# Left-over rows of each expert in 32-row fp32 tails beside the 128-row slots

## The reference

```
c0   = per-batch 64x64 mix of x + bias               (stage 0, "cond")
logits = c0 @ gate_w                                  (8 experts)
top 2 experts of each row, softmax over the two logits -> w0, w1
x1   = x + w0 * (c0 @ expert_w[e0]) + w1 * (c0 @ expert_w[e1])     (1024 x 1024 each)
c1   = grouped convolution of x1 (9 taps) + bias      (stage 2)
out  = x1 + c1 @ weight.T + gated LoRA of c1          (stage 2)
```

## Time and profile before

| | |
|---|---|
| median of the runs | 840.09 us |
| profiled execution | 842.59 us, of which the span is 840.8 us |
| mean granted TensorE clock | 0.995 |
| TensorE matmul busy | 820.3 us (98%) |
| VectorE / ScalarE / GpSimd busy | 399.5 / 216.5 / 86.8 us |
| slot and main product, L1353 | 848 low-row matmuls = 53 x 16 |
| DMA | 149.32 MB, mean 178 GB/s |

### The profile page before, as it was taken

The page is one execution under the profiler, slowest core; times in us unless marked ns, Lnnn a source line. Parts: engine busy times, 40 slices in busy tenths (PEclk is TensorE's granted clock), DMA queues, the critical chain, the costliest instruction groups (busy, mean ns, idle before and its releaser), DMA issues.

```text
span 840.8 us, 12876 instructions
## 1 busy us (share of the span) xinstructions
PE 820.3 (98%) x4286; PEld 678.5 (81%) x4287; DVE 399.5 (48%) x919; ACT 216.5 (26%) x335; POOL 86.8 (10%) x136
## 2 busy tenths in 40 slices
PE   8999899999999999999999999999999999999997
PEld 6555588888888888888888888789888888988886
DVE  1388750251513304233042150466766776777883
ACT  2344341342524314243142251310001000101200
POOL 1000111011101111011101112021111111110000
PEclk9999999999999999999999999999999999999999
DMA  9998489373554634546255253584564456432056
GB/s 288 351 325 308 178 291 417 121 253 134 168 194 169 217 100 162 200 138 248 80 179 202 87 184 108 189 257 102 137 149 114 103 144 151 101 84 67 1 196 204
DMA packets 61801, 149.32 MB, mean 178 GB/s; under 512 B 6944, under 2 KB 23600, under 8 KB 60848
## 3 DMA queue, kind: packets, MB, share of 16 engines
q1 hardware_dynamic: 41104, 93.41, 33.7%
q0 software_dynamic: 9968, 36.19, 14.7%
q10 hardware_dynamic: 10704, 19.41, 6.1%
HBM read 100.74 MB, written 39.85 MB: 167 GB/s over the span
## 4 chain that ended last, share of the span: by engine, by line
PE 85%; DMA 6%; DVE 3%; issue 2%; ACT 2%; SPq 1%; ACTq 1%; POOL 0%; DVEq 0%; POOLq 0%
PE bank L1353 60%; PE bank L1392 6%; PE bank L1248 4%; PE bank L1401 4%; PE bank L1344 3%; DMA work<-in_expert_w 3%; PE bank L1408 3%; PE bank L1225 1%; DVE weights L977 1%; DMA work<-y_scratch,pos_c 1%; PE bank L1297 1%; PE bank L1272 1%; PE bank L1211 1%; DMA x1p<-res 1%; PE bank L1237 1%
## 5 line engine op out<-in xcount | busy, mean ns | idle before, releaser
L1353 PE MATMUL bank<-weights,l_hi 128*128 128x512 f32 x1696 | 524.4, 391 | 0.0
L1353 PEld LDWEIGHTS bank<-weights,l_hi 128*128 128x128 f32 x1696 | 319.4, 188 | 64.8
L1353 PE MATMUL bank<-weights,l_lo 128*128 128x512 f32 x848 | 336.1, 396 | 2.0 <-DVE l_lo L945 2.0
L1353 PEld LDWEIGHTS bank<-weights,l_lo 128*128 128x128 f32 x848 | 159.8, 188 | 34.7 <-issue 3.4
L945 DVE TENSOR_TENSOR l_lo<-bank,l_hi 128x512 fp32r<-128x512 f32 x37 | 25.6, 691 | 183.7 <-ACT l_hi L715 183.7
L977 DVE TENSOR_TENSOR weights<-work,weights 128x1024 fp32r<-128x1024 f32 x64 | 76.2, 1222 | 50.8 <-ACT weights L726 50.0
L726 ACT ACTIVATE weights<-work 128x1024 fp32r<-128x1024 f32 x64 | 65.3, 1055 | 41.9 <-DMA work<-in_expert_w 23.6
L572 POOL DMA_INDIRECT work<-c_scratch,idx x37 | 40.5, 1094 | 291.7 <-PE bank L1344 198.9
L1392 PE MATMUL bank<-conv_sb,x1p 128*128 128x128 f32 x512 | 59.8, 276 | 3.8 <-DMA x1p<-work 2.6
L1392 PEld LDWEIGHTS bank<-conv_sb,x1p 128*128 128x128 f32 x512 | 58.7, 192 | 4.3 <-DMA x1p<-work 2.8
L950 DVE TENSOR_TENSOR l_lo<-bank,l_hi 128x512 fp32r<-128x512 f32 x37 | 25.6, 691 | 68.7 <-ACT l_hi L720 68.7
(11 more groups left out here) (184 smaller groups left out, 528.9 us busy)
## 6 DMA issues: line engine op xcount, KB each, us to landing
work<-in_expert_w SPq DMA_DIRECT2D x68, 512.0 KB, 6.4
y_scratch<-work ACTq DMA_DIRECT2D x74, 256.0 KB, 2.1
res<-in_x SPq DMA_DIRECT2D x16, 512.0 KB, 15.3
c_scratch<-work SPq DMA_DIRECT2D x16, 512.0 KB, 3.5
res<-in_x_ph SPq DMA_DIRECT2D x14, 512.0 KB, 5.6
x1p<-res SPq DMA_DIRECT2D x112, 64.0 KB, 4.7
out<-res SPq DMA_DIRECT2D x14, 512.0 KB, 5.3
work<-in_x_t SPq DMA_DIRECT2D x6, 1024.0 KB, 7.3
```

The source lines that it names most:

```text
L1353: mm = pe.matmul(to[:, :], a[:, k, :], b[:, k, cols * HALF:(cols + 1) * HALF], start=(k == 0 and n == 0), stop=(k == HC - 1 and n == 2 and ...
```

## The change

Experts 2 to 7 ("grouped", six of them; experts 0 and 1 are "plain") may leave up to 32 rows out of their slots. These go into a tail of 32 rows. The number of slots of a grouped expert is now what it takes to hold its rows less 32, with at least two for each expert (three for the last). All six tails are always computed.

- The 6 x 32 tail rows are gathered once (two indirect DMAs), turned by TensorE behind expert 0 (`turn_tails`, 16 transposes), and copied to `tail_xt` by ScalarE and VectorE. They stay in full fp32.
- A tail's product takes the weights as loaded from `raw`, in fp32, in `tail(e, half)`: for each of the four chunks of the half, four matmuls of 32 stationary and 256 moving columns, which write the four groups of 32 partitions of one bank. Eight chunks make 32 matmuls.
- `experts_slot`: behind the first slot of expert `e`, TensorE runs `tail(e + 1, 0)` and then `tail(e + 1, 1)`.
- SyncE does not start the second half of expert `e + 1` until `tail(e + 1, 0)` is done, nor the first half of `e + 2` until `tail(e + 1, 1)` is done. Within a half it now waits for the converted chunks one by one.
- ScalarE takes a tail's result out of bank 4 and stores it (`take_tail`), behind `round_w(e, odd, 1)`.
- The fill of unused rows of `y_scratch` moves behind the loads of experts 1 to 4; it grows, since `SLOTS` is 46 instead of 39. `x_first` is loaded behind the last tail. The four zero fills of `x1p` on GpSimd move behind the turned tails.
- TensorE's expert loop is written out over experts 1 to 7.

```diff
+LEAST = [2] * (E - 1) + [3]
+SLOTS = 2 * NT + (E - 2) * 2 + 2
+FILLS = 4
+TAIL, PLAIN = 32, 2
+GROUPED = E - PLAIN
...
+        tail_xt = row(6, 2)[:, 0:GROUPED * HC * TAIL].rearrange("p (i k m) -> p i k m", i=GROUPED, k=HC)
+        tail_x = [x1p[j][:, :, :, :].rearrange("p b u w -> p (b u w)")[:, 0:H] for j in range(2)]
...
# SyncE
+            def load_raw(e, half, free=None):
                 for k in range(HC // 2):
+                    if free is not None:
+                        sp.wait_ge(s_lo, free + (k + 1))
                     sp.dma_start(raw[k], expert_w[e, half * (HC // 2) + k, :, :].rearrange("o p n -> p (o n)")).then_inc(s_raw[k], 16)
...
-                sp.wait_ge(s_lo, (e + 1) * HC + HC // 2)
-                load_raw(nxt, 1)
+                if not first and not last:
+                    wait_apart(sp, s_tprod, e * 2 - 1)
+                load_raw(nxt, 1, (e + 1) * HC)
                 if between is not None:
                     between()
                 if not last:
-                    sp.wait_ge(s_lo, (e + 1) * HC + HC)
-                    load_raw(nxt2, 0)
+                    if not first:
+                        wait_apart(sp, s_tprod, e * 2)
+                    load_raw(nxt2, 0, (e + 1) * HC + HC // 2)
...
+            for part in range(FILLS):
+                with sp.Fori(1 + part, 2 + part) as e:
+                    expert(e, False, False)
+                fill(part)
...
# ScalarE
+            def take_tail(e):
+                act.wait_ge(s_tprod, e * 2)
+                act.wait_ge(s_tst, e * 16)
+                act.activation(tail_out, bank[4][:, 0:H // QUAD], ACT.Copy).then_inc(s_tev, 1)
+                wait_apart(act, s_tev, e)
+                behind = act.value_load(cum[0:1, bass.ds(e + 2, 1)], min_val=PLAIN, max_val=SLOTS)
+                rows = bass.ds(act.snap(behind * P + e * TAIL), TAIL)
+                act.dma_start(y_d[rows, :].rearrange("r (g n) -> g r n", g=QUAD), tail_out).then_inc(s_tst, 16)
...
# VectorE, slots of an expert
+            ch.link(dve.scalar_tensor_tensor(cmp[:, PLAIN:E, :], bank[4][:, PLAIN:E]...,
+                                             float(-TAIL), c("thr")..., ALU.add, ALU.is_gt))
...
# TensorE
+            def turn_tails():
+                pe.wait_ge(s_tgot[1], 16)
+                rows = (GROUPED - QUAD) * TAIL
+                for k in range(HC):
+                    mm = pe.transpose(bank[6][:, k * rows:(k + 1) * rows], tail_x[1][0:rows, k * P:(k + 1) * P], ...)
+                mm.then_inc(s_tturn, 1)
+                pe.wait_ge(s_tgot[0], 16)
+                for k in range(HC):
+                    mm = pe.transpose(bank[4 + k // 4][:, k % 4 * P:(k % 4 + 1) * P], tail_x[0][:, k * P:(k + 1) * P], ident)
...
+            def tail(e, half):
+                if e == PLAIN and half == 0:
+                    for turned_in in s_txt:
+                        pe.wait_ge(turned_in, 1)
+                elif half == 0:
+                    pe.wait_ge(s_tev, e - PLAIN)
+                for n in range(HC // 2):
+                    k = half * (HC // 2) + n
+                    pe.wait_ge(s_raw[n], (e - 1) * 32 + (half + 1) * 16)
+                    for g in range(QUAD):
+                        mm = pe.matmul(bank[4][g * TAIL:(g + 1) * TAIL, 0:H // QUAD], tail_xt[:, e - PLAIN, k, :],
+                                       raw[n][:, g * (H // QUAD):(g + 1) * (H // QUAD)], start=(k == 0), stop=(k == HC - 1))
+                mm.then_inc(s_tprod, 1)
+
+            def experts_slot(g, e, odd, first):
+                tailed = first and PLAIN <= e + 1 < E
+                slot(g, e, odd, first)
+                if tailed:
+                    tail(e + 1, 0)
+                    tail(e + 1, 1)
+
+            one_expert(pe, experts_slot, 0, 0)
+            turn_tails()
+            for e in range(1, E):
+                one_expert(pe, experts_slot, e, e % 2)
```

More of the change, by code:

```diff
@@ L328, in build @@
         s_rest = sem("s_rest")
+        s_tplace = sem("s_tplace")
+        s_tidx = sem("s_tidx")
+        s_tgot = [sem(f"s_tgot_{j}") for j in range(2)]
+        s_tturn = sem("s_tturn")
+        s_txt = [sem(f"s_txt_{j}") for j in range(3)]
+        s_tprod = sem("s_tprod")
+        s_tev = sem("s_tev")
+        s_tst = sem("s_tst")
         s_ctx0 = sem("s_ctx0")
@@ L362, in build, with one_expert, places @@
         program = ctx.enter_context(nc.Block())
[L364 to L374, removed]
+        def one_expert(eng, body, e, odd):
+            first = eng.value_load(cum[0:1, bass.ds(e, 1)], min_val=0, max_val=SLOTS - 1)
+            end = eng.value_load(cum[0:1, bass.ds(e + 1, 1)], min_val=1, max_val=SLOTS)
+            second = eng.snap(first + 1)
+            body(first, e, odd, True)
+            with eng.Fori(second, end) as g:
+                body(g, e, odd, False)
+        def places(e):
+            return max(e - 1, 0) * TAIL if isinstance(e, int) else e * TAIL - TAIL
         def turned(it):
@@ L465, in late_loads @@
                 sp.wait_ge(s_const, 16)
[L466 to L467 removed]
+                behind = sp.value_load(cum[0:1, PLAIN:PLAIN + 1], min_val=sum(LEAST[:PLAIN]), max_val=SLOTS)
+                sp.dma_start(y_d[bass.ds(sp.snap(behind * P), TAIL), :], ca[0:TAIL, 0:H]).then_inc(s_rest, 16)
                 sp.dma_start(cb[:, :], consts_b).then_inc(s_late, 16)
@@ L629, in _ @@
             fetch(0)
-            second = pool.value_load(near[0:1, 0:1], min_val=E, max_val=SLOTS)
-            wait_apart(pool, s_y0, second * 16 + DMA_CREDIT)
-            wait_apart(pool, s_y1, second * 16 + DMA_CREDIT)
+            wait_apart(pool, s_y0, (begun + 2) * 16 + DMA_CREDIT)
+            wait_apart(pool, s_y1, (begun + 2) * 16 + DMA_CREDIT)
             fetch(1)
@@ L752, in slot @@
                     round_w(e, odd, 1)
-            slots(act, slot)
+                    if not isinstance(e, int):
+                        take_tail(e)
+            one_expert(act, slot, 0, 0)
+            act.wait_ge(s_tturn, 2)
+            act.activation(tail_xt[:, 0:QUAD, 0:HC // 2, :], bank[4][:, :].rearrange("p (k i m) -> p i k m", k=HC // 2, i=QUAD),
+                           ACT.Copy).then_inc(s_txt[1], 1)
+            with act.Fori(0, GROUPED // 2) as pair:
+                for odd in (1, 0):
+                    one_expert(act, slot, pair * 2 + 2 - odd, odd)
+            one_expert(act, slot, E - 1, 1)
             act.wait_ge(s_x1f, 2)
@@ L989, in _ @@
             dve.wait_ge(s_lo, HC)
[L990 to L1000, removed]
+            one_expert(dve, slot, 0, 0)
+            dve.wait_ge(s_tturn, 1)
+            dve.tensor_copy(tail_xt[:, QUAD:GROUPED, :, :], bank[6][:, :].rearrange("p (k i m) -> p i k m", k=HC, i=GROUPED - QUAD)).then_inc(s_txt[0], 1)
+            dve.wait_ge(s_tturn, 3)
+            dve.tensor_copy(tail_xt[:, 0:QUAD, HC // 2:HC, :],
+                            bank[5][:, :].rearrange("p (k i m) -> p i k m", k=HC // 2, i=QUAD)).then_inc(s_txt[2], 1)
+            with dve.Fori(0, GROUPED // 2) as pair:
+                for odd in (1, 0):
+                    one_expert(dve, slot, pair * 2 + 2 - odd, odd)
+            begun = dve.value_load(cum[0:1, E - 1:E], min_val=sum(LEAST[:-1]), max_val=SLOTS - LEAST[E - 1])
+            end = dve.value_load(cum[0:1, E:E + 1], min_val=sum(LEAST), max_val=SLOTS)
             rest_w(E - 1, 1, 0)
-            with dve.Fori(dve.snap(last_b + 1), second) as g:
-                rest_a(g)
-                rest_b(g)
+            rest_a(dve.snap(begun + 1))
+            rest_b(dve.snap(begun + 1))
             rest_w(E - 1, 1, 1)
-            with dve.Fori(second, end) as g:
+            with dve.Fori(dve.snap(begun + 2), end) as g:
                 rest_a(g)
```

102 lines of the change are left out of this document (71 added, 31 removed).

## The result

The changed kernel takes 869.7 us, the median of four runs (865.96 to 873.16), against 840.15 us for the kernel before in the same series. The ratio is 1.033, with an interval of 1.031 to 1.036: slower, where 871 us was forecast. In microseconds that is 27.8 by the ratio (25.6 to 30.0), 29.6 between the two medians and 27.2 between the two profiled executions; +31.2 was forecast. The profiled execution took 869.8 us with a span of 868.0 us.

The account below looks back on a forecast made before the run. TensorE, busy 98% of the span, was taken to bound the kernel. The terms -47.1 + 23.5 + 41 + 12 + 1.8 = +31.2 us on 840.1 gave 871 us, 3.7% slower, range 855 to 888.

Parts of the forecast that it names:

- four slots fewer: Stage 1: experts 3, 5, 6 and 7 take four slots instead of five, 37 becomes 33, 47.1 us less.
- products: TensorE's 32 fp32 matmuls a tail, priced from stage 0's gate products at 3.92 us, 23.5 us more.
- wait for the second half: Between a tail's halves TensorE idles for a 2 MB load, 6.8 us a tail, 41 us more (36 to 56).
- clock: Each tail's wait drops TensorE to 1.2 GHz, 2.0 us lost a tail, 12 us more (0 to 24).
- turning the tails: Behind expert 0: 16 transposes on TensorE, eight of them short, 1.8 us more.
- two allowances of 0.3 us: In the load wait: 0.3 us for SyncE seeing the semaphore, 0.3 for issues with register addresses standing further apart.
- the row it rested on: Stage 1's start before the change: two TensorE gaps around transposes, then 3.3 us at half speed, 1.65 us lost.
- nothing else is due from ScalarE then: At `take_tail`: ScalarE blocks until the tail is done, claimed free because the next slot's rows were already split.
- prices beside the chosen one: Other estimates of a tail's products: 4.5 us by the skill's column-group speedup, 14.4 us if matmuls don't run side by side.

Follow-up runs that it names:

- halves apart: Against the changed kernel, each tail's second half moved behind the running expert's second slot, ScalarE's taking of the tail too; 819.5 us, ratio 0.970.
- gaps filled: Against the changed kernel, constant matmuls added between each tail's halves and behind the second half's first three chunks; 859.6 us, ratio 1.020.
- experiment without the load between: Against the changed kernel, each tail's second half reread the first half's chunks, with the load behind both (wrong result); 845.1 us, ratio 1.003.

## Why the prediction was right

By its own steps, in us over the whole kernel:

| step | forecast | measured | by |
|---|---|---|---|
| four slots fewer | -47.1 | -47.1 | 784 records; transposes 11.78 apart |
| products | +23.5 | +22.4 | twelve halves of 1.87 (halves apart) |
| wait for the second half | +41 | +39.4 | 6 x (7.94 + 0.49 - 1.87) |
| clock | +12 | +11.4 to 11.8 | gaps filled; 6 x (1.38 + 0.59) |
| turning the tails | +1.8 | +1.7 | 16 transposes, 163.82 to 165.49 |
| sum | +31.2 | +27.8 | ratio 1.033 |

The slots and the four positive terms make 27.8 to 28.2 by their measured values, so no large term is missing. The wait was the term that had to be right, since it turns a gain of 3% into a loss of 3%, and it came from one batch of loads in the trace before, in which the last of four landed 7.7 us behind the first issue. In the changed kernel four tails took 7.6 to 7.7 us from the first half's end and two took 8.5 and 8.7. The two allowances of 0.3 us on top of the batch were mostly not needed: the first issue stands 0.1 us behind the half's end in all six tails (358.83 to 358.92, for one), and in that tail the four issues take 1.79 us, as in the batch alone (1.76).

The clock step was right in its mechanism and partly by luck in its size and in its support. Forecast were 1.65 us in the slot behind and 0.35 in the last chunk's products, measured 1.38 and 0.59. And the row it rested on did not repeat: at the start of stage 1 of the changed kernel TensorE idles 2.18 us, transposes for 1.07, idles 1.06, nearly as in the earlier trace rows, and the clock stays at 1.00. Gaps of that size are a doubtful base; what the six tails have is a first gap of 3.8 to 5.0 us.

```profile
100.26 1.07 PE L1438 MATMUL bank<-ca,work 128*128 128x128 f32 x8 [2.18 <-DMA work<-c_scratch,idx]
102.39 0.47 PE L1447 MATMUL bank<-weights,l_lo 128*128 128x512 f32 x1 [1.06 <-DVE l_lo L1036]
...
103.00:104.00 1.00, 1.00 (x6) 0.84 (x5) 0.82 (x5) 0.02 (x1) 0.92 (x1) 1.00 1.05 426
```

Small things went other ways and nearly cancelled. Stage 0 was 1.1 us longer in the profiled run. With the clock up in the first slot, 1.65 us were not lost there, but the next slot's rows came late by 2.09 us, where nothing had been forecast: their gather started 1 us later than before and took 7.2 us. A gather for the last expert's second slot took 10.6 us and cost 0.7. Stage 2's first main product began 1.5 us sooner after the first convolution, since the second convolution waited 1.16 us for its rows instead of 2.64; which of the changes did that was not tried. That these cancel is luck.

Where the prediction was weaker than its number: "nothing else is due from ScalarE then" holds only because TensorE waits too. The experiment without the load between showed that ScalarE's rounding of the late half and taking of the tail, with VectorE's part behind them, have a second price of about 26 us, hidden behind the wait. In the kernel with the halves apart it just fits: VectorE ends the split rows at 189.95 (from 189.26), and TensorE wants them at 190.33.

```profile
185.39 1.06 ACT L794 ACTIVATE weights<-work 128x1024 fp32r<-128x1024 f32 x1 [0.20 <-DMA work<-in_expert_w]
186.36 0.58 ACT L820 ACTIVATE work<-bank 128x512 f32<-128x512 f32 x1
...
189.26 0.69 DVE L1053 TENSOR_TENSOR l_lo<-bank,l_hi 128x512 fp32r<-128x512 f32 x1 [0.33 <-ACT l_hi L788]
```

The prices beside the chosen one for a tail's products, 3.92 us, were too high: 4.5 us for the groups in turn, where 3.74 was measured, and 14.4 us with the groups not side by side, where neighbours in one group took 9.1.

The rule named beside the clock step (the Trainium skill, "TensorE: Matmul & The Clock Gate", HAM oscillation: waits for a DMA between short groups of matmuls start each group cold) agrees with the trace: the clock fell in all six waits, to 1.2 GHz, and the products of a chunk took 1.08 us instead of 0.64; keeping it up gave back 11.4 us.

## What to carry to other kernels

When a saving needs a buffer twice, ask what the engine that bounds the kernel does between the two uses. A release and a refill that stand next to each other in its program cost the whole load each time (7.9 us for 2 MB here), whatever the saving is; with one slot of other work between them the same change went from 3% slower to 3% faster.

If such a wait can't be moved, work that nobody needs gives back the clock's part of it, and only that (11.4 of 50 us), and filling the long gap alone gave back less (4.5 us) than filling most of the short ones too. And when one wait is taken away, read which in-order engine stood behind it: here ScalarE took the second slot's result over 6 us late, TensorE waited 3 us a tail for it, and half of the gain was gone.

## What the runs showed of the hardware

- Matmuls of 32 stationary and 256 moving columns in fp32 run at 0.058 us a record when neighbours stand in four different column groups, and at 0.142 us when eight in a row stand in one group; a full-width record of 256 columns would take 0.225, an estimate from the earlier trace rows.
- The clock fell in gaps of 3.8 to 5.0 us in all six tails, and, with the first gap filled, in two of six tails, whose longest gaps were 0.97 and 0.65 us. With the short gaps filled as well it stayed at 2.4 GHz in all six, though a gap of up to 1.46 us ahead of the first chunk was left.
- The same kernel part gave either level: idle times of 2.06 and 1.16 us around 1.06 us of transposes ended at 1.2 GHz before the change, idle times of 2.18 and 1.06 around 1.07 us did not after it.
- Loads issued 0.5 us apart, as soon as their buffers were free, landed 0.2 us sooner on average than when all four were issued together, the first of them 1.3 us later (first half of a tail to last chunk 9.7 against 9.9 us).
- Taking and storing a tail's 256 columns held ScalarE for 2.7 us (245.81 to 248.53), of which its arithmetic is 0.36.
